# The last eleven token scatters of a routed-expert loop, spread over 22 tiles and not over 16

## The chip, the cores and the metric

The kernel runs on one core of one Trainium2 chip. The metric is device time in microseconds (us) of one execution. Three runs of the kernel before took 496.35, 493.66 and 497.1 us, a median of 496.35 us. The profile is of one further execution.

## What is computed

The reference is one decoder layer on 64 x 64 tokens of width 128: self-attention with 8 heads, an mLSTM cross step against a context, and a mixture-of-experts feed-forward, each added to its input and normalised. The change touches the last of them alone, which is:

```python
for i in range(E_SHARED):
    shared_out = shared_out + _expert(x, shared_up[i], shared_down[i])
probs = jax.nn.softmax(jnp.einsum('bsh,he->bse', x, router_w), axis=-1)
top_k_prob, top_k_idx = jax.lax.top_k(probs, K)          # K = 2 of 8 experts
onehot = jax.nn.one_hot(top_k_idx, E_ROUTED, dtype=x.dtype)
gates = jnp.einsum('bsk,bske->bse', top_k_prob, onehot)
for e in range(E_ROUTED):
    y = _expert(x, routed_up[e], routed_down[e])         # gelu(x @ up) @ down
    routed_out = routed_out + gates[..., e:e + 1] * y
return shared_out + routed_out + x
```

All tensors are float32; an expert's weights are 128x512 and 512x128.

## The kernel before

The 4096 tokens are 32 tiles of 128. Each token goes to two experts, so there are 8192 token copies. The kernel sorts them by expert through memory. **Scatter** n (n from 0 to 63, function `scatter`, line 471) is one indirect DMA from GpSimd (POOL in the profile): it takes the 128 rows of token tile n // 2 (130 numbers each: the token, its gate and its destination; from `tkr`, or from a copy in `zbuf` for odd n) and writes them to their places in a buffer `slots` in device memory. It raises one of four semaphores `scat`, by the quarter of the tokens it belongs to. Scatters 0 to 52 are issued in the stages ahead, the last of them during the shared expert. The remaining eleven, 53 to 63, belong to the last quarter and are issued inside the routed loop.

The **routed loop** runs over 71 expert tiles (`SLOT_TILES`), each 128 rows of `slots` that belong to one expert. A table worked out from the counts of the first half of the tokens picks the first 24 tiles (`EARLY`) so that they hold tokens of scatters 0 to 31 alone. The other 47 need all scatters. The engines do for tile t:

- SyncE (SP): wait until the row scatter of tile t - 8 has landed (semaphores `sc_y`), read the tile's place from a table, load 128 rows of `slots` into one of eight buffers `xr` (they lie in `zbuf`; lines 338 and 339). Ahead of tile 24 it waits at line 360 for all 16 scatters of each of the last two quarters.
- TensorE (PE): step t is a transpose of tile t (`turn`, line 1315, into `pair` or a bank), then four up matmuls of tile t - 1 (`up`, line 1323), then four down matmuls of tile t - 2 (`down`, line 1333), in this order. Each float32 matmul is two in the trace, hence x8. `turn` of tile t waits for the load of tile t.
- VectorE (DVE): copy the expert's up weights to `wst` (line 1802; `prob` in the trace), copy the transposed tile out (line 1795), then scale the output of tile t - 2 by its gates (`y_out`, line 1808). The up matmuls of a tile need the first two.
- ScalarE (ACT): gelu (line 894), which the down matmuls need.
- GpSimd: once `y_out` of tile t is done, the **row scatter** of tile t (`rows_out`, line 574), an indirect DMA of 128 rows of 128 numbers to `routed`.

GpSimd executes in the order of the program. So the order of row scatters and token scatters on it is what the Python code writes out: a straight part of 16 tiles (`2 * NX`, NX = 8), then a hardware loop for the rest. After the loop the final stage reads `routed`, adds and normalises.

Of the kernel before, what the change touches and what calls it, by code (L numbers as in the profile page):

```python
# [14 lines left out]
NT = B * S // P  # L15
# [10 lines left out]
SLOT_TILES = FILL_TILES - 1  # L26
EARLY = 24
IN_B = 21
IN_LOOP = IN_B + 32
# [38 lines left out]
def decoder_layer(nc, x, ctx_in, w_qk, w_v, w_out, b_out, conv, w_ig, b_ig, w_fg, b_fg, ln_w,  # L68
# [153 lines left out]
    NX = 8  # L222
# [160 lines left out]
    def _(pool):  # L383
# [81 lines left out]
        def scatter(n):  # L465
            t, k = n // 2, n % 2
            g = t // GT
            if n % (2 * GT) == 0:
                pool.wait_ge(s["slot_ok"], g // 2 + 1)
                pool.wait_ge(s["tk_ok"], 16 * (g + 1))  # L470
            pool.indirect_dma_start(slots, bass.IndirectOffsetOnAxis(ap=slot[:, k, t:t + 1], axis=0),  # L471
                                    (tkr, tk1)[k][:, t, :], None).then_inc(scat[g // 2], 16)
# [99 lines left out]
        def rows_out(t, n):  # L572
            pause(pool, s["y_ok"], t + 1, s["passed_pool"])
            pool.indirect_dma_start(routed, bass.IndirectOffsetOnAxis(ap=xr[n][:, :].bitcast(I32)[:, DEST:DEST + 1], axis=0),  # L574
                                    yr[n % 4][:, :], None).then_inc(sc_y[n % 4], 16)
        for t in range(2 * NX):
            rows_out(t, t % NX)
            if t % 3 < 2 and IN_LOOP + t - t // 3 < 2 * NT:
                scatter(IN_LOOP + t - t // 3)
        with pool.Fori(2, SLOT_TILES // NX) as i:  # L580
            for n in range(NX):
                rows_out(NX * i + n, n)
        for n in range(SLOT_TILES % NX):
# [1312 lines left out]
```

## Time and profile before

| | |
|---|---|
| median of three runs | 496.35 us |
| profiled execution | 495.9 us, of which the span from first to last instruction is 493.7 us |
| TensorE, matmul busy | 459.5 us, 93% |
| VectorE | 309.5 us, 63% |
| ScalarE | 277.9 us, 56% |
| GpSimd | 184.8 us, 37% |
| mean granted TensorE clock | 0.977 of full |

The page of the profile gives for each engine the busy time. The engine names are PE (matmul), PEld (its weight loads, which run beside matmuls), DVE, ACT, POOL and SP. The routed loop lies between about 305 and 467 us of the span. All times below are us from the span's start.

### The profile page before, as it was taken

To read this page: it belongs to the slowest core of one execution; us is meant where nothing else is said; L and a number is where in the kernel's file an instruction comes from. 1 tells how busy PE (TensorE), PEld (TensorE's weight loads), DVE (VectorE), ACT (ScalarE), POOL (GpSimd) and SP (SyncE) were. 2 spreads that over 40 slices of the span, in tenths; PEclk is the share of its full clock that TensorE was granted. 3 is DMA by queue.
4 is the path that set the end of the run, shared out by engine and by line. 5 is a ranking of instruction groups with operands and counts; after the bars stand their busy time and mean duration, and the time that the engine had idled before them with its cause. 6 is when DMAs were issued, how large, how long until landed. Compare 5 with 4: busy or idle time off the path is not lost.

```text
span 493.7 us, 15314 instructions
## 1 busy us (share of the span) xinstructions
PE 459.5 (93%) x5214; PEld 389.1 (79%) x5215; DVE 309.5 (63%) x1002; ACT 277.9 (56%) x624; POOL 184.8 (37%) x209
## 2 busy tenths in 40 slices
PE   8999999999998999989889999788899999999984
PEld 7688888887786777766579999777799999999631
DVE  5578888888885678888665672333344544455246
ACT  5687867786666989887678542112122332222226
POOL 5512011117000111156656464565545555555300
PEclk9999999999998999999979999898899999999999
DMA  5343136500000161111112123121222222222186
GB/s 140 88 120 99 53 97 132 156 1 4 24 5 19 37 222 45 45 50 56 56 56 70 39 70 90 58 63 60 60 67 65 65 65 69 59 70 60 53 288 203
DMA packets 47879, 37.98 MB, mean 77 GB/s; under 512 B 5456, under 2 KB 41184, under 8 KB 47824
## 3 DMA queue, kind: packets, MB, share of 16 engines
q1 hardware_dynamic: 43072, 28.10, 20.8%
q0 software_dynamic: 4320, 8.92, 5.1%
q8 instruction: 37, 0.61, 0.5%
q10 hardware_dynamic: 432, 0.20, 0.1%
q14 instruction: 18, 0.15, 0.1%
HBM read 19.30 MB, written 16.34 MB: 72 GB/s over the span
## 4 chain that ended last, share of the span: by engine, by line
PE 55%; DVE 21%; ACT 9%; issue 7%; DMA 3%; another core or an unknown queue 2%; DVEq 2%; SPq 0%; POOL 0%; ACTq 0%; POOLq 0%
PE bank L1333 12%; PE bank L1323 12%; PE bank L1283 6%; DVE tkr L1445 2%; DVE negmax L1454 2%; DVE prob L1451 2%; PE bank L1007 2%; PE bank L954 2%; DMA wdn<-routed 2%; PE bank L956 2%; PE bank L955 2%; PE bank L997 2%; PE pair L1315 1%; DVE stats L1593 1%
## 5 line engine op out<-in xcount | busy, mean ns | idle before, releaser
L894 ACT ACTIVATE prob<-bank 128x512 f32<-128x512 f32 x71 | 42.2, 597 | 121.3 <-PE bank L1323 106.8
L574 POOL DMA_INDIRECT routed<-zbuf x71 | 73.6, 1036 | 72.1 <-DVE zbuf L1808 40.3
L1323 PE MATMUL bank<-cT,prob 128*128 128x128 f32 x568 | 78.9, 283 | 8.9 <-DVE prob L1802 7.9
L1333 PE MATMUL bank<-wdn,prob 128*128 x568 | 80.6, 287 | 1.7 <-ACT prob L894 1.5
L1323 PEld LDWEIGHTS bank<-cT,prob 128*128 128x128 f32 x568 | 71.2, 197 | 12.2 <-DVE prob L1802 9.9
L1333 PEld LDWEIGHTS bank<-wdn,prob 128*128 128x128 f32 x568 | 71.4, 197 | 2.9 <-issue 2.2
L1802 DVE COPY prob<-wup 128x512 f32 x71 | 30.6, 430 | 44.6 <-issue 25.4
L1808 DVE TENSOR_SCALAR zbuf<-bank,zbuf 128x128 f32<-128x128 f32 x71 | 24.9, 350 | 46.0 <-PE bank L1333 29.6
L471 POOL DMA_INDIRECT slots<-zbuf,slot x32 | 31.4, 981 | 20.8 <-PE bank L1283 7.6
L471 POOL DMA_INDIRECT slots<-tkr,slot x32 | 31.5, 986 | 13.9 <-issue 6.4
L461 POOL TENSOR_TENSOR hlw<-hst,lnw 128x512 f32<-128x512 f32 x8 | 10.2, 1275 | 63.2 <-ACT hst L784 63.2
L1283 PEld LDWEIGHTS bank<-sdn,qblk 128*128 128x128 f32 x256 | 30.1, 194 | 0.6
L1283 PE MATMUL bank<-sdn,qblk 128*128 128x128 f32 x256 | 30.1, 277 | 0.0
L607 ACT ACTIVATE prob<-prob 128x512 f32<-128x512 f32 x32 | 20.2, 631 | 14.7 <-DVE prob L1455 14.6
L954 PE MATMUL bank<-xT_hi,wq_hi 128*128 128x512 f32 x64 | 27.9, 436 | 0.0
L1180 PEld LDWEIGHTS bank<-vals,cmat 64*64 64x64 f32 x512 | 17.6, 134 | 10.4 <-issue 10.4
L956 PE MATMUL bank<-xT_lo,wq_hi 128*128 128x512 f32 x64 | 25.4, 397 | 0.0
L955 PE MATMUL bank<-xT_hi,wq_lo 128*128 128x512 f32 x64 | 25.1, 393 | 0.0
L1451 DVE TENSOR_TENSOR prob<-pair,bias 128x512 f32<-128x512 f32 x32 | 22.0, 688 | 4.0 <-PE pair L977 2.7
L1455 DVE TENSOR_TENSOR prob<-prob,negmax 128x512 f32<-128x512 f32 x32 | 23.3, 728 | 1.1
L1160 PE MATMUL bank<-qblk,cT 128*64 128x256 f32 x128 | 21.0, 405 | 2.5 <-DVE cmat L1554 1.9
L1180 PE MATMUL bank<-vals,cmat 64*64 64x33 f32 x512 | 20.7, 222 | 2.8 <-issue 2.2
(281 smaller groups left out, 995.0 us busy)
## 6 DMA issues: line engine op xcount, KB each, us to landing
slots<-x2T SPq DMA_DIRECT2D x8, 585.0 KB, 5.3
zbuf<-slots SPq DMA_DIRECT2D x71, 65.0 KB
tkr<-in_x SPq DMA_DIRECT2D x8, 256.0 KB, 2.9
cs<-in_ctx SPq DMA_DIRECT2D x8, 256.0 KB, 2.8
wup<-in_L_ffn_routed_up SPq DMA_DIRECT2D x1, 2048.0 KB, 8.7
zbuf<-tkr SPq DMA_DIRECT2D x8, 256.0 KB
wup<-routed SPq DMA_DIRECT2D x8, 256.0 KB, 3.6
wdn<-routed SPq DMA_DIRECT2D x8, 256.0 KB, 4.0
```

The source lines that it names most:

```text
L471: pool.indirect_dma_start(slots, bass.IndirectOffsetOnAxis(ap=slot[:, k, t:t + 1], axis=0), (tkr, tk1)[k][:, t, :], None).then_inc(scat[g ...
L574: pool.indirect_dma_start(routed, bass.IndirectOffsetOnAxis(ap=xr[n][:, :].bitcast(I32)[:, DEST:DEST + 1], axis=0), yr[n % 4][:, :], None) ...
L894: act.activation(hT[:, n % 2, :], bank[2 + n % 2][:, :], ACT.Gelu).then_inc(s["hT_ok"], 1)
L954: mm(bank[4 + h % 2][:, :], wq_hi[:, h, :], xh[:, :], start=True, stop=False)
L955: mm(bank[4 + h % 2][:, :], wq_lo[:, h, :], xh[:, :], start=False, stop=False)
L956: mm(bank[4 + h % 2][:, :], wq_hi[:, h, :], xl[:, :], start=False, stop=True).then_inc(s["z_ps"], 1)
L1180: m = mm(bank[5 + k // 2][r, c:c + 33], cmat[r, k % 2, h * S:(h + 1) * S], vals[q][r, k, h, :], start=True, stop=True)
L1283: m = mm(bank[4 + g % 2][:, k * D:(k + 1) * D], shT[g % 2][:, c, k * P:(k + 1) * P], sdn[:, c, :], start=(c == 0), stop=(c == FC - 1))
L1323: m = mm(bank[2 + n % 2][:, c * P:(c + 1) * P], wst[:, n % 2, c * P:(c + 1) * P], xrT[:, n % 2, :], start=True, stop=True)
L1333: m = mm(bank[6 + n % 2][:, 0:D], hT[:, n % 2, c * P:(c + 1) * P], wdn[:, bass.ds(e * (FC * D) + c * D, D)], start=(c == 0), stop=(c == FC ...
L1451: tt(prob[:, k, :].rearrange("p (e x) -> p e x", e=2), pair[:, :, 0:256], bias[:, :, :].rearrange("p (e c) j -> p e (c j)", e=2), ALU.add) ...
L1802: dve.tensor_copy(wst[:, n % 2, :], wup[:, bass.ds(e * FF, FF)]).then_inc(s["wst_ok"], 1)
```

## The change

The straight part of the GpSimd program is 24 tiles long, and a token scatter stands behind the row scatters of tiles 0, 2, 4, ... 20. Before, it was 16 tiles long with token scatters behind the row scatters of tiles 0, 1, 3, 4, 6, 7, 9, 10, 12, 13 and 15. The scatters, their number and their data are the same.

```diff
-        for t in range(2 * NX):
+        for t in range(3 * NX):
             rows_out(t, t % NX)
-            if t % 3 < 2 and IN_LOOP + t - t // 3 < 2 * NT:
-                scatter(IN_LOOP + t - t // 3)
-        with pool.Fori(2, SLOT_TILES // NX) as i:
+            if t % 2 == 0 and IN_LOOP + t // 2 < 2 * NT:
+                scatter(IN_LOOP + t // 2)
+        with pool.Fori(3, SLOT_TILES // NX) as i:
```

What stands in the GpSimd program at the start of the routed loop, before (-) and now (+). L574 is a row scatter, L471 a token scatter; "x2" is two in a row.

```order
 L574 DMA routed<-zbuf 9344x128 [waits y_ok]
 L471 DMA slots<-zbuf,slot 43008x130
-L574 DMA routed<-zbuf 9344x128 [waits y_ok]
+L574 DMA routed<-zbuf 9344x128 [waits y_ok] x2
 L471 DMA slots<-tkr,slot 43008x130
 L574 DMA routed<-zbuf 9344x128 [waits y_ok] x2
 L471 DMA slots<-zbuf,slot 43008x130
```

Before, a pair of token scatters had one row scatter between them and two ahead of the next pair. Now two row scatters stand between any two token scatters. The same at the last two token scatters, 62 and 63:

```order
-L574 DMA routed<-zbuf 9344x128 [waits y_ok]
+L574 DMA routed<-zbuf 9344x128 [waits y_ok] x2
 L471 DMA slots<-tkr,slot 43008x130
 L574 DMA routed<-zbuf 9344x128 [waits y_ok] x2
 L471 DMA slots<-zbuf,slot 43008x130
+L574 DMA routed<-zbuf 9344x128 [waits y_ok] x3
 L580 UNCONDITIONAL_BRANCH
```

The last row but two was behind tile 15's row scatter and is now behind tile 20's; three row scatters (21 to 23) follow ahead of the hardware loop. The program of SyncE is the same in both. This is its place between tile 23 and tile 24 (rows of the changed kernel), where the last token scatter is waited for:

```order
L339 DMA zbuf<-slots 128x130
L341 REGISTER_ALU
L341 COMPARE_AND_BRANCH
L341 UNCONDITIONAL_BRANCH [waits scat2,scat3,st_pad,toff_ok]
L341 ISA
L338 ISA [waits sc_y0]
```

The load ahead of the wait is that of tile 23, and the one behind it is tile 24's; the wait did not move, but one of the things it waits for did.

## Rows read from the trace of the kernel before

**Rows 1.** Timeline, DVE, line 1808 (y_out), tiles 1, 2, 4, 6, 16, 20, 70.

```profile
310.38 0.35 DVE L1808 TENSOR_SCALAR zbuf<-bank,zbuf 128x128 f32<-128x128 f32 x1 [0.43 <-PE bank L1333]
...
315.34 0.35 DVE L1808 TENSOR_SCALAR zbuf<-bank,zbuf 128x128 f32<-128x128 f32 x1 [3.46 <-PE bank L1333]
...
320.02 0.35 DVE L1808 TENSOR_SCALAR zbuf<-bank,zbuf 128x128 f32<-128x128 f32 x1 [2.15 <-PE bank L1333]
...
325.65 0.35 DVE L1808 TENSOR_SCALAR zbuf<-bank,zbuf 128x128 f32<-128x128 f32 x1 [1.39 <-PE bank L1333]
...
355.18 0.35 DVE L1808 TENSOR_SCALAR zbuf<-bank,zbuf 128x128 f32<-128x128 f32 x1 [2.58 <-issue]
...
363.04 0.35 DVE L1808 TENSOR_SCALAR zbuf<-bank,zbuf 128x128 f32<-128x128 f32 x1 [0.45 <-PE bank L1333]
...
463.47 0.35 DVE L1808 TENSOR_SCALAR zbuf<-bank,zbuf 128x128 f32<-128x128 f32 x1 [1.00 <-PE bank L1333]
```

**Rows 2.** Stretches: from:to, length; busy PE, PEld, DVE, ACT, POOL; clock, DMA share, GB/s.

```profile
296.00:310.00 14.00, 13.63 (x115) 13.15 (x114) 4.22 (x11) 3.75 (x7) 6.34 (x8) 1.00 0.34 86
310.38:355.18 44.80, 35.74 (x257) 34.00 (x256) 14.54 (x46) 8.74 (x15) 26.10 (x27) 0.89 0.20 60
355.18:463.47 108.29, 107.19 (x909) 104.23 (x908) 51.38 (x158) 32.94 (x54) 55.53 (x54) 1.00 0.22 63
317.70:321.10 3.40, 3.40 (x19) 3.40 (x18) 0.75 (x3) 0.60 (x1) 1.92 (x2) 0.50 0.26 80
```

**Rows 3.** Timeline, POOL: start us, length us, instruction, idle time before it and releaser.

```profile
310.90 0.96 POOL L471 DMA_INDIRECT slots<-zbuf,slot  x1 [0.31 <-DVE zbuf L1808]
312.17 0.96 POOL L574 DMA_INDIRECT routed<-zbuf  x1 [0.30 <-issue]
313.43 0.96 POOL L471 DMA_INDIRECT slots<-tkr,slot  x1 [0.30 <-issue]
...
321.16 0.96 POOL L574 DMA_INDIRECT routed<-zbuf  x1 [1.07 <-issue]
322.43 0.95 POOL L471 DMA_INDIRECT slots<-tkr,slot  x1 [0.30 <-issue]
323.69 1.21 POOL L574 DMA_INDIRECT routed<-zbuf  x1 [0.30 <-issue]
326.79 1.07 POOL L574 DMA_INDIRECT routed<-zbuf  x1 [1.90 <-DVE zbuf L1808]
```

**Rows 4.** Timeline, PE, around tiles 2 to 10.

```profile
311.18 1.06 PE L1333 MATMUL bank<-wdn,prob 128*128 x8
...
316.91 1.36 PE L1323 MATMUL bank<-cT,prob 128*128 128x128 f32 x8 [2.67 <-DVE prob L1802]
...
326.18 1.15 PE L1333 MATMUL bank<-wdn,prob 128*128 x8 [0.69 <-ACT prob L894]
```

**Rows 5.** Groups by line, DVE alone, 310.38 to 355.18 and 355.18 to 463.47.

```profile
L1802 DVE COPY prob<-wup 128x512 f32 x15 | 6.5, 436 | 8.1 <-issue 8.1
...
L1802 DVE COPY prob<-wup 128x512 f32 x52 | 22.3, 429 | 34.6 <-PE bank L1323 18.4 <-issue 16.1
```

**Rows 6.** Timeline, POOL: token scatter 63, row scatters of tiles 16 and 20.

```profile
353.74 0.95 POOL L471 DMA_INDIRECT slots<-zbuf,slot  x1 [0.30 <-issue]
356.32 1.06 POOL L574 DMA_INDIRECT routed<-zbuf  x1 [1.63 <-DVE zbuf L1808]
...
364.18 1.06 POOL L574 DMA_INDIRECT routed<-zbuf  x1 [0.96 <-issue]
```

**Rows 7.** SP: line 360 (duration min/median/max ns, starts), and the load of tile 24.

```profile
L360 SPq EVENT_SEMAPHORE  x2: 17/22/28, 356.1 to 356.4; - x2
...
359.55 0.26 SPq L339 DMA_DIRECT2D zbuf<-slots  x1
```

**Rows 8.** Issues of DMAs: KB, median us from issue to landing.

```profile
wv<-in_L_attn_W_v ACTq DMA_DIRECT2D x1, 64.0 KB, 1.9
```

**Rows 9.** Timeline, PE: the transpose of tile 24.

```profile
364.66 0.28 PE L1315 MATMUL pair<-ident,zbuf 128*128 128x128 f32 x1
```

## The prediction

> **What bounds the kernel now.** I read the busy time by stretch first. From 355.18 to 463.47 TensorE is busy for 107.19 of 108.29 us at the full clock (1.00, which is 2.4 GHz): the routed loop is bound by TensorE [rows 2]. The starts of y_out give its pace: tile 16 at 355.18 and tile 70 at 463.47, 54 tiles in 108.29 us, 2.0 us each [rows 1]. From 310.38 to 355.18, tiles 1 to 16, it is not: TensorE is busy for 35.74 of 44.80 us at a mean clock of 0.89 [rows 2]. Fifteen tiles at 2.0 us would take 30.1 us, so **14.7 us are lost** there. They split into 9.1 us without a matmul (44.80 - 35.74) and the half clock: a mean of 0.89 means 22% of the stretch at 0.5 (1.2 GHz), 9.9 us, in which half the work is done, 4.9 us. The row of 317.70 to 321.10 is one of three such pieces, and it follows the wait of 2.67 us before 316.91 [rows 2, 4]. This stretch is the one in which GpSimd has token scatters between its row scatters: 27 DMAs for 16 tiles.
>
> The timelines show how the two hang together. GpSimd starts DMAs 1.26 us apart when it never waits (310.90, 312.17, 313.43; 321.16, 322.43, 323.69) [rows 3]. Before the change five of them fall on three tiles: 6.3 us of GpSimd for 6.0 us of TensorE, so it is overbooked. And in such runs the consumers learn late that TensorE is done. Tile 2's down matmuls, from 311.18 for 1.06 us, end at 312.24, but y_out of tile 2 starts at 315.34 after 3.46 us of idle time put down to just these matmuls [rows 1, 4]. The next weight copy stands behind it on VectorE, and TensorE then waits 2.67 us for that copy. What holds the signal back the profile doesn't name. Ahead of the loop, where token scatters have gaps, TensorE is busy for 13.63 of 14.00 us [rows 2]. So the loss comes with runs of GpSimd DMAs without a gap, or with the token scatters among them; which, the change will tell.
>
> **The change part by part.** Nothing is added or removed; eleven DMAs of about 1 us move. Two terms follow.
>
> *Term 1, the stretch with scatters.* Three DMAs for two tiles are 3.8 us of GpSimd for 4.0 us of TensorE: it just keeps up. But each group is still a row scatter, a token scatter and a row scatter without a gap. Such a group exists before: 321.16, 322.43, 323.69, then a gap of 1.90 us [rows 3]. From y_out of tile 4 to that of tile 6 it takes 5.63 us where two tiles take 4.0: 1.6 us lost, of which TensorE shows 0.69 as a wait [rows 1, 4]. The rest may be left from the half clock just before, so the price of one group lies between 0.69 and 1.6; I take the middle, 1.15. Below 0.69 the bound is nothing at all, if the group was only hit because GpSimd came to it late; above, 1.6. Ten groups cost 11.5 us; the eleventh falls into the wait of term 2. Term 1 is 11.5 - 14.7 = **-3.2 us**.
>
> One rule of the Trainium skill bears on the cause. "SBUF — State Buffer", section "Who interferes with whom", says that a VectorE copy in a two-port mode and GpSimd lock each other out for a whole instruction, descriptor writing included. If that were the loss, each scatter would hold one weight copy for up to its own 1 us, the count of scatters being the same the loss would stay, and the sum would be that of the rival "as costly as now". By the rows the copies are not held: 436 ns in the stretch with token scatters and 429 ns in the one without [rows 5].
>
> *Term 2, tile 24.* SyncE waits ahead of the load of tile 24 for all token scatters. Before, scatter 63 starts at 353.74 and the wait at line 360 ends at 356.4, 2.7 us later; the load isn't held by it, since it waits for tile 16's row scatter anyway (356.32) and goes out at 359.55, 3.2 us after that started [rows 6, 7]. Now scatter 63 stands behind tile 20's row scatter. With y_out of tile 20 as zero: its row scatter starts at 1.14 (363.04 to 364.18), scatter 63 at 2.40 (1.26 later), the load goes out 3.2 us after (the same chain of landing, table read and issue), at 5.6, and lands 1.9 us later, by the nearest row of 64 KB, at 7.5 [rows 1, 3, 6 to 8]. The transpose of tile 24 stood at 364.66 - 363.04 = 1.6 [rows 1, 9]. It is late by **5.9 us**. It stands first in step 24, so the up matmuls of tile 23 and the down matmuls of tile 22 wait behind it although their data is there, and then gelu, y_out and the row scatters. Nothing hides it: TensorE has no idle time behind it in which to catch up [rows 2]. The loads of tiles 25 to 28 are late too, but by then their row scatters have landed and SyncE issues them in a row; I take it that each comes ahead of its 2.0 us and adds nothing. The wait is longer than the 2.67 us that was followed by 3.4 us at half clock, so I add one such piece, **1.7 us**. Term 2 is **+7.6 us**. Its bounds: the load may land in less (1.9 is a transfer at the kernel's start, 1.5 possible, an estimate), and the clock may not fall or fall for two pieces: 5.5 to 9.3.
>
> In "DMA: Bandwidth & Descriptors", section "Anatomy of one DMA — SWDGE (gpsimd) path", the Trainium skill gives a GpSimd DMA about 2.0 us plus bytes / 436e3, an estimate of 2.15 us for these 66,560 bytes. By it tile 24 would be late by some 0.5 us less; the row's 2.7 us decides.
>
> *Sum.* The profiled execution took 495.9 us (span 493.7), 0.45 below the median of 496.35. 495.9 - 3.2 + 7.6 = **500.3 us**.
>
> **The rivals.**
> *Relief, the other side.* If GpSimd's being overbooked is the sole cause, then 3.8 us in 4.0 us ends it, no group costs anything, and the whole 14.7 us come back: 495.9 - 14.7 + 7.6 = **488.8 us**, faster. For it: where token scatters had gaps TensorE did not wait. Against: the group at 321.16 came after a gap of 1.07 us and had its loss nonetheless [rows 3]. It decides from a price below some 0.2 us a group: 14.7 - 10 x 0.2 - 7.6 = 5.
> *Half relief.* A group costs the 0.69 us that TensorE shows: 495.9 - 14.7 + 6.9 + 7.6 = **495.7 us**, no change.
> *As costly as now.* Each token scatter costs what it does now, 14.7 / 11 = 1.34 us, wherever it stands: -14.7 + 13.4 + 7.6 gives **502.2 us**; at 1.6 us a group 504.8.
> *The wait at tile 24 is hidden.* Were TensorE so late by the groups that tile 24's load had come, term 2 would vanish: 492.7 us. Against it: what delays TensorE delays y_out of tile 20, from which the 7.5 us count. So hardly.
>
> **How the numbers follow.** Forecast 0.37 (497 to 502), as costly as now 0.27 (to 505), half relief 0.19 (493 to 497), relief 0.13 (487 to 492), hidden wait 0.04. The likeliest gives 500.3. The range reaches into relief and over the costly case: 490 to 506. A measurement of this kernel can tell about 1% from no change, so the borders are 491.4 and 501.3. Slower takes most of the costly case and a third of the forecast: 0.38. Faster takes relief and a bit of the hidden wait: 0.16. Same keeps 0.46.
>
> **What would show it.** In the changed profile TensorE must have one wait of 5 to 6 us ahead of the transpose of tile 24, ended by the load, whose issue comes about 3.2 us after token scatter 63; after it a piece at clock 0.50. Between y_out of tiles 1 and 20 the time over 2.0 us a tile must be near 11 us, without pieces at half clock, in waits of about 1 us, one for each token scatter. If it is near 0, relief is right and GpSimd's booking is the cause; if near 13 or more with pieces at half clock, the token scatters themselves cost. No wait at tile 24 would make term 2 wrong, and with it the sign.

## The result, and the profile after

The changed kernel took 498.9 us (median of 20 runs) beside 494.1 us for the kernel before (20 runs): a ratio of **1.0083, 95% interval 1.0059 to 1.0108**. It is slower, by 4.8 us between the medians (4.1 us by the ratio), where the prediction had +4.4; 498.9 us lies between the borders of 491.4 and 501.3 us within which the prediction counted a time as no change. The ratio leaves out three runs of the changed kernel that lay over 1.5% above its fastest. The profiled execution has a span of 497.4 us where before had 493.7.

Starts of y_out (line 1808) of tiles 1, 20, 23 in the changed kernel's timeline of VectorE; they answer to [rows 1]:

```profile
310.51 0.35 DVE L1808 TENSOR_SCALAR zbuf<-bank,zbuf 128x128 f32<-128x128 f32 x1 [0.43 <-PE bank L1333]
...
359.88 0.35 DVE L1808 TENSOR_SCALAR zbuf<-bank,zbuf 128x128 f32<-128x128 f32 x1 [1.25 <-PE bank L1333]
...
374.07 0.35 DVE L1808 TENSOR_SCALAR zbuf<-bank,zbuf 128x128 f32<-128x128 f32 x1 [0.48 <-PE bank L1333]
```

From tile 1 to tile 20 it takes 49.37 us; before took 363.04 - 310.38 = 52.66 us [rows 1]. So the stretch with token scatters is **3.3 us shorter**. Then the sign turns. The busy time by stretch, cut at these tiles and at tile 70 (467.31); from:to, length, busy PE, PEld, DVE, ACT, POOL, clock, DMA share, GB/s, as in [rows 2]:

```profile
310.51:359.88 49.37, 39.08 (x327) 37.08 (x326) 18.09 (x57) 11.24 (x19) 28.22 (x30) 1.00 0.20 60
359.88:374.07 14.19, 7.92 (x52) 7.70 (x51) 3.03 (x10) 1.79 (x3) 4.74 (x5) 0.76 0.18 52
374.07:467.31 93.24, 92.66 (x790) 90.29 (x789) 44.57 (x138) 28.77 (x47) 48.35 (x48) 1.00 0.22 63
365.50:372.30 6.80, 4.44 (x21) 4.41 (x22) 1.01 (x3) 0.60 (x1) 0.83 (x1) 0.50 0.24 60
```

The first stretch has TensorE idle for 10.3 of 49.37 us, all of it at the full clock. The second has three tiles in 14.19 us. The last one is bound by TensorE, as before. The fourth row is the piece at half clock (0.50) inside the second stretch. From tile 20 to tile 70 it takes 107.43 us where before took 463.47 - 363.04 = 100.43 us [rows 1]: **7.0 us longer**. The two add up to +3.7 us, which is the difference of the spans. All of the 7.0 us and a little more arises in the three tiles: before took 6.61 us from tile 20 to tile 23 (y_out of tile 23 starts at 369.65 in its trace) and 93.82 us from there to tile 70, now it is 14.19 and 93.24 us, so +7.6 and -0.6 us.

The row that makes the second stretch is in the timeline of TensorE, the transpose of tile 24, answering to [rows 9]:

```profile
367.86 0.47 PE L1315 MATMUL pair<-ident,zbuf 128*128 128x128 f32 x1 [6.27 <-DMA zbuf<-slots]
368.12 2.03 PE L1323 MATMUL bank<-cT,prob 128*128 128x128 f32 x8
369.95 1.92 PE L1333 MATMUL bank<-wdn,prob 128*128 x8
```

It waited 6.27 us for a load, and the eight matmuls behind it take 2.03 and 1.92 us where they take 1.06 at the full clock [rows 4]. The chain of work that ended last, in the order of time (start, length, what), tells where the load was:

```profile
361.02 1.07 POOL routed L574
362.09 0.30 issue
362.40 2.33 DMA slots<-zbuf,slot
...
364.75 0.03 SPq L360
...
365.82 1.91 DMA zbuf<-slots
...
367.86 0.47 PE pair L1315
```

It is the chain of the prediction link by link: tile 20's row scatter, token scatter 63, its landing, the wait at line 360, the load, the transpose. In the waits of SyncE (line, what it waited for: us in total, times, longest) line 360 had 0.3 us before and now has:

```profile
SPq L360 <- DMA slots<-zbuf,slot: 11.2, 1, 11.2
```

The first stretch looks like this on GpSimd; the rows answer to [rows 3]:

```profile
315.22 0.95 POOL L574 DMA_INDIRECT routed<-zbuf  x1 [1.96 <-DVE zbuf L1808]
316.48 0.96 POOL L471 DMA_INDIRECT slots<-tkr,slot  x1 [0.30 <-issue]
317.75 0.96 POOL L574 DMA_INDIRECT routed<-zbuf  x1 [0.31 <-issue]
319.86 0.96 POOL L574 DMA_INDIRECT routed<-zbuf  x1 [1.14 <-issue]
321.12 0.99 POOL L471 DMA_INDIRECT slots<-zbuf,slot  x1 [0.30 <-issue]
322.41 0.96 POOL L574 DMA_INDIRECT routed<-zbuf  x1 [0.30 <-issue]
```

Groups of three, 1.26 us apart, each followed by a gap. And TensorE has a wait for nearly every group; that of the second group is

```profile
320.43 1.15 PE L1323 MATMUL bank<-cT,prob 128*128 128x128 f32 x8 [0.75 <-DVE cT L1795]
```

There are eight such waits of 0.59 to 2.17 us for the ten groups, 10.3 us together.

### The profile page after: what moved, and what is told of

It reads as the page before. It is cut to its first block, busy times and chain, and to the rows that moved or that the text cites. A ratio compares the mean times of both kernels' runs of the same rounds, so it can differ in the third digit from the quotient of the medians.

```text
span 497.4 us, 15304 instructions
## 1 busy us (share of the span) xinstructions
PE 457.9 (92%) x5214; PEld 386.6 (78%) x5215; DVE 309.6 (62%) x1002; ACT 278.4 (56%) x624; POOL 184.2 (37%) x209
## 4 chain that ended last, share of the span: by engine, by line
PE 54%; DVE 19%; ACT 9%; issue 7%; DMA 5%; another core or an unknown queue 2%; DVEq 2%; POOL 1%; SPq 1%; ACTq 0%; POOLq 0%
PE bank L1323 12%; PE bank L1333 11%; PE bank L1283 6%; DMA wdn<-routed 3%; DVE negmax L1454 2%; DVE prob L1451 2%; PE bank L1007 2%; PE bank L954 2%; DVE tkr L1445 2%; PE bank L956 2%; PE bank L955 2%; PE bank L997 2%; PE pair L1315 1%; DVE prob L1455 1%
## 5 line engine op out<-in xcount | busy, mean ns | idle before, releaser
L574 POOL DMA_INDIRECT routed<-zbuf x71 | 73.2, 1031 | 76.1 <-DVE zbuf L1808 48.5
L1323 PE MATMUL bank<-cT,prob 128*128 128x128 f32 x568 | 77.7, 281 | 8.9 <-DVE prob L1802 5.6
L1333 PE MATMUL bank<-wdn,prob 128*128 x568 | 78.8, 282 | 2.3 <-ACT prob L894 2.2
L1323 PEld LDWEIGHTS bank<-cT,prob 128*128 128x128 f32 x568 | 70.1, 194 | 12.3 <-DVE prob L1802 7.3
L1333 PEld LDWEIGHTS bank<-wdn,prob 128*128 128x128 f32 x568 | 69.7, 193 | 3.3 <-issue 2.7
L471 POOL DMA_INDIRECT slots<-zbuf,slot x32 | 31.5, 985 | 21.2 <-PE bank L1283 7.6
L471 POOL DMA_INDIRECT slots<-tkr,slot x32 | 31.2, 976 | 13.6 <-issue 6.3
L607 ACT ACTIVATE prob<-prob 128x512 f32<-128x512 f32 x32 | 20.2, 631 | 14.7 <-DVE prob L1455 14.6
L1315 PE MATMUL pair<-ident,zbuf 128*128 128x128 f32 x71 | 19.6, 279 | 6.3 <-DMA zbuf<-slots 6.3
```

What stands on the lines that cost most here:

```text
L1323: m = mm(bank[2 + n % 2][:, c * P:(c + 1) * P], wst[:, n % 2, c * P:(c + 1) * P], xrT[:, n % 2, :], start=True, stop=True)
L1333: m = mm(bank[6 + n % 2][:, 0:D], hT[:, n % 2, c * P:(c + 1) * P], wdn[:, bass.ds(e * (FC * D) + c * D, D)], start=(c == 0), stop=(c == FC ...
```

## The experiments

One thing has to be told ahead, since no number below can be read without it. The runs were made in several sessions, and the kernel before took 494 us in some and 477 us in others, within about 1% of its median inside a session (but for one run of it of 1475.66 us, beside extra_gaps). In the runs behind the prediction and the comparison above it took 494 to 496. I call the first the *slow condition* and the second the *quick condition*. All times are compared within their session. Nothing on record says what sets the condition; it is not the chip's number, since chip 9 showed both. There is no trace of the kernel before in the quick condition, so its order is read there from kernels that share it. The two conditions turned out to be an experiment of their own.

### Only the last scatter moved

The kernel before, with scatter 63 behind tile 20 and not behind tile 15:

```diff
-        for t in range(2 * NX):
+        at = [0, 1, 3, 4, 6, 7, 9, 10, 12, 13, 20]
+        for t in range(3 * NX):
             rows_out(t, t % NX)
-            if t % 3 < 2 and IN_LOOP + t - t // 3 < 2 * NT:
-                scatter(IN_LOOP + t - t // 3)
-        with pool.Fori(2, SLOT_TILES // NX) as i:
+            if t in at:
+                scatter(IN_LOOP + at.index(t))
+        with pool.Fori(3, SLOT_TILES // NX) as i:
```

> The order of before, except that the last token scatter, 63, stands behind tile 20's row scatter and not behind tile 15's. Two-term theory: the wait at tile 24 comes by this one move. TensorE waits 5.5 to 6.5 us ahead of the transpose of tile 24, followed by one or two pieces at half clock, and the kernel takes 6 to 8 us more than before, less the 1.3 us that scatter 63 costs at tile 15: +5 to +7 us. Rival (the wait at tile 24 is made by all eleven scatters being late, or by the longer straight part of the GpSimd program): less than 2 us more than before.

Measured, quick condition: 485.5 beside 477.15 us, ratio 1.0185 (1.0131 to 1.0239), +8.4 us (four runs of this kernel). TensorE's timeline at the transpose of tile 24 (its line is 1316 here):

```profile
355.10 0.47 PE L1316 MATMUL pair<-ident,zbuf 128*128 128x128 f32 x1 [6.33 <-DMA zbuf<-slots]
```

The busy time of each engine in two stretches of the same kernel, tiles 1 to 16 and the piece behind the wait (columns as above):

```profile
308.99:339.08 30.09, 30.09 (x258) 29.38 (x257) 14.87 (x45) 8.96 (x15) 22.77 (x25) 1.00 0.29 81
...
355.10:359.90 4.80, 4.80 (x22) 4.76 (x23) 0.64 (x2) 0.60 (x1) 0.00 (x0) 0.50 0.24 56
```

The wait comes by this one move. The size was missed upwards: 4.8 us at half clock behind it are 2.4 us, and the 1.3 us that I had taken off for scatter 63 were not there. The first stretch says why: fifteen tiles in 30.09 us, with TensorE never idle, in the *order of before* but for scatter 63. The 14.7 us lost there by [rows 1, 2] are absent in the quick condition.

### The changed kernel in the quick condition

> The changed kernel itself beside before, on whatever chip this runs. In the last runs before took 477 us where it took 494 to 496 in the runs of the comparison, and no TensorE signal came late there, before's fifteen tiles 1 to 16 taking 2.0 us each. Theory: the 14.7 us lost in the stretch with token scatters belong to the chip or its state, and the wait at tile 24 belongs to the order. So where before takes some 477 us, the changed kernel takes 6 to 8 us more (1.3 to 1.7%), all of it at tile 24, and where before takes some 495 us it takes 3 to 5 more (0.6 to 1.0%). Rival (both terms change together by the chip): the ratio is 1.008 in either case.

Measured: 485.1 beside 476.7 us, ratio 1.0173 (1.0135 to 1.021), +8.4 us (four runs), a little above the expected 6 to 8. The stretches of this kernel from tile 1 to 20 and from 20 to 23:

```profile
309.21:346.99 37.78, 37.78 (x326) 37.03 (x325) 18.73 (x58) 11.35 (x19) 28.29 (x30) 1.00 0.27 79
346.99:360.54 13.55, 7.54 (x52) 7.29 (x51) 3.03 (x10) 1.79 (x3) 4.41 (x5) 0.75 0.20 54
```

The transpose of tile 24 in its timeline of TensorE:

```profile
354.75 0.47 PE L1315 MATMUL pair<-ident,zbuf 128*128 128x128 f32 x1 [6.01 <-DMA zbuf<-slots]
```

So the two terms separate. The wait at tile 24 belongs to the order and is there in both conditions. The loss at token scatters, and with it all that the spacing can win, belongs to the slow condition. The rival with one ratio for both is out: the intervals of 1.0173 and 1.0083 don't touch.

### The spacing without the wait

Against the changed kernel ("..." marks lines left out, here and below):

```diff
+        for n in range(2):
+            scatter(IN_LOOP + n)
+        at = list(range(0, 17, 2))
...
-            if t % 2 == 0 and IN_LOOP + t // 2 < 2 * NT:
-                scatter(IN_LOOP + t // 2)
+            if t in at:
+                scatter(IN_LOOP + 2 + at.index(t))
```

> Two token scatters (53, 54) go out ahead of tile 0's row scatter, where GpSimd idles for 3.6 us, and the other nine behind the row scatters of tiles 0, 2, ... 16. So the spacing is that of the changed kernel but the last scatter is out by tile 16. Two-term theory: no wait at tile 24; nine groups at about 1.15 us are 10 us where 14.7 us were lost before: -4 to -5 us against before (-0.9%). Relief theory (GpSimd overbooked is all): no loss, -14 us. Rival that spacing gains nothing: within 1 us of before less two scatters' 1.3 us each, -2.6 us.

Measured, quick condition: 476.7 beside 477.15 us, ratio 0.9984 (0.9959 to 1.0009): no difference. With nothing lost at token scatters there is nothing to win: its tiles 1 to 16 take 29.88 us. With the last one at tile 16 there is no wait: from y_out of tile 20 (346.95) to that of tile 23 (353.53) it takes 6.58 us, where before took 6.61 and the changed kernel 13.55 in this condition. The expectation of -4 us was made without the condition in mind and fell with it.

### How far back the last scatter may stand

The kernel before, with scatter 63 behind tile 18. The edit is that of last_at_20 with another last number:

```diff
+        at = [0, 1, 3, 4, 6, 7, 9, 10, 12, 13, 18]
...
```

> As last_at_20, but scatter 63 stands behind tile 18's row scatter. Every tile is 2.0 us, so the wait ahead of the transpose of tile 24, 6.3 us with the scatter at tile 20, is to be 4.0 us shorter: 2.3 us, with about one piece at half clock after it at most. Two-term theory: +2 to +4 us against before, and the wait ends by the load of tile 24. Rival (the wait isn't a chain from scatter 63 but a fixed cost of the scatter being in the third group of eight tiles): 6 us of wait again.

Measured, slow condition: 497.4 beside 494.4 us, ratio 1.0035 (0.9994 to 1.0076), an interval that holds 1: the times alone tell no difference, and the trace carries this one. The transpose of tile 24 in its timeline of TensorE:

```profile
370.02 0.33 PE L1316 MATMUL pair<-ident,zbuf 128*128 128x128 f32 x1 [1.90 <-DMA zbuf<-slots]
```

Two tiles earlier, the wait is 1.90 us where it is 6.0 to 6.3, so 4.1 to 4.4 us shorter for 4.0 us of two tiles. It is a chain from the scatter, not a fixed cost. By the same slope of 2.0 us a tile it would be gone with the scatter at tile 17; that is an estimate and was not run.

### The clock behind the wait

The changed kernel, with 26 matmuls that nobody reads (a filler) ahead of the loop from tile 24 on:

```diff
         pe.wait_ge(s["toff_ok"], 2)
+        pe.wait_ge(s["base_ok"], NG)
+        filler(4, 26)
```

> The changed kernel with 26 identity matmuls of 128 x 128 into an unused bank ahead of the transpose of tile 24, some 5.8 us of TensorE work that lies in the wait for the load and computes nothing that is used. The wait itself stays (the tile comes when the load does), but TensorE has no idle time in it. If the half clock behind the wait is a cost of its own: 1.7 to 2.4 us less than the changed kernel, which takes 8.4 us more than before on this chip, so +6 to +7 us. If the half clock costs nothing: +8.4 us or more.

Measured, slow condition: 497.6 beside 494.4 us, ratio 1.0064 (1.0033 to 1.0094). The filler is 5.97 us of TensorE work at line 932. TensorE's timeline between tile 20 and the transpose of tile 24:

```profile
359.05 5.97 PE L932 MATMUL bank<-ident 128*128 128x128 f32 x52
366.08 0.33 PE L1315 MATMUL pair<-ident,zbuf 128*128 128x128 f32 x1 [1.06 <-DMA zbuf<-slots]
366.31 1.15 PE L1323 MATMUL bank<-cT,prob 128*128 128x128 f32 x8
```

The stretch of this kernel from y_out of tile 20 to that of tile 23:

```profile
358.28:370.52 12.24, 11.18 (x97) 10.72 (x96) 2.93 (x10) 1.80 (x3) 3.63 (x4) 1.00 0.18 51
```

12.24 us where the changed kernel has 14.19, and the clock stays at 1.00. The transpose starts 7.80 us after y_out of tile 20 and not 7.98, so 0.2 us of the difference is a load that came sooner, and the half clock behind the wait is a cost of its own of some 1.8 us; the rest of term 2 is the wait. The expected +6 to +7 us was reckoned from the quick condition. Here it is +3.1 us, where the comparison had +4.8; the ratio, against 1.0083, points the same way, but the two intervals overlap; the trace carries this one. From tile 1 to tile 20 this kernel takes 49.25 us, against 49.37 in the changed kernel's own profile: term 1 repeats.

### All token scatters ahead, without gaps

Against the kernel before: every scatter from a point ahead of the shared expert on stands there in one row, without the waits between them, and none is left in the loop.

```diff
-        first = IN_B
-        pool.wait_ge(s["shu_ps"], FC + 2)
-        scatter(first)
-        pool.wait_ge(s["x2T_ps"], NG - 1)
-        scatter(first + 1)
...
-        pool.wait_ge(s["shd_ps"], NG)
-        scatter(IN_LOOP - 1)
+        for n in range(IN_B, 2 * NT):
+            scatter(n)
...
-        for t in range(2 * NX):
-            rows_out(t, t % NX)
-            if t % 3 < 2 and IN_LOOP + t - t // 3 < 2 * NT:
-                scatter(IN_LOOP + t - t // 3)
-        with pool.Fori(2, SLOT_TILES // NX) as i:
+        with pool.Fori(0, SLOT_TILES // NX) as i:
```

> All token scatters from 21 on without waits on TensorE's progress between them, one behind the other at 1.26 us from about 255 us on; the eleven late ones are out before tile 0's row scatter. Where TensorE's signals don't come late (before at some 477 us): nothing to win in the loop, which runs at 2.0 us a tile already, and nothing lost, within 2 us of before; if GpSimd isn't done when tile 0 is, its row scatter is late by a few us and the first tiles wait, +1 to +4 us. Where they come late (before at some 495 us): the loop wins 14 us, and the shared expert ahead of it loses 5 us or more.

Measured, slow condition: 522.1 beside 494.4 us, ratio **1.0554** (1.0489 to 1.0619). The busy time in three stretches of this kernel, the shared expert's first and second part, then tiles 1 to 16:

```profile
255.00:309.00 54.00, 34.93 (x203) 28.91 (x202) 14.18 (x48) 20.43 (x33) 26.58 (x28) 0.73 0.12 39
309.00:350.71 41.71, 31.35 (x219) 28.71 (x218) 16.15 (x53) 9.28 (x16) 16.59 (x17) 0.88 0.20 52
350.71:380.48 29.77, 29.77 (x258) 29.32 (x257) 14.71 (x45) 8.98 (x15) 15.62 (x16) 1.00 0.23 66
```

The kernel before over nearly the same time:

```profile
255.00:308.00 53.00, 52.63 (x397) 48.97 (x396) 28.72 (x97) 28.88 (x47) 31.09 (x33) 0.99 0.23 65
```

There TensorE is busy nearly without a break; in this kernel it is idle for a third of the time. The third row is the other half of the finding: with no token scatter left in it, the loop runs its fifteen tiles in 29.8 us, in the slow condition. From 255.46 on GpSimd issues 27 token scatters in a row; its timeline at one place:

```profile
281.02 0.96 POOL L471 DMA_INDIRECT slots<-zbuf,slot  x1 [0.30 <-issue]
282.28 0.96 POOL L471 DMA_INDIRECT slots<-tkr,slot  x1 [0.30 <-issue]
```

TensorE's timeline just behind it:

```profile
284.42 0.58 PE L1201 MATMUL pair<-wq_hi,xT_hi 128*128 128x512 f32 x1 [2.44 <-issue]
288.05 0.59 PE L1202 MATMUL pair<-wq_hi,xT_lo 128*128 128x512 f32 x1 [3.05 <-issue]
290.84 0.59 PE L1203 MATMUL pair<-wq_lo,xT_hi 128*128 128x512 f32 x1 [2.20 <-issue]
```

And ScalarE's, for the instruction that reads what these matmuls wrote:

```profile
293.99 1.09 ACT L837 ACTIVATE qblk<-pair 128x512 f32<-128x512 f32 x2 [8.80 <-PE pair L1203]
```

GpSimd issues without a gap, and three matmuls that add into the same bank, with no wait between them in the code, start 3.6 and 2.8 us apart, with "issue" before them, which says that the profile knows nothing they waited for. ScalarE idles for 8.80 us, from 285.19 on. For 6.2 us of it TensorE itself is late, since the third of these matmuls ends only at 291.43 (290.84 + 0.59); the other 2.6 us pass between that end and ScalarE's start.

A late signal shows more clearly near the head of the same row, in one instruction of VectorE, the copy of the router's result. In the code it waits for the router's matmuls. First in the kernel before, then here, where those matmuls lie 0.24 us later:

```profile
261.25 0.19 DVE L1573 COPY lg<-bank 128x32 f32<-128x32 f32 x1 [4.34 <-PE bank L1195]
...
266.93 0.19 DVE L1552 COPY lg<-bank 128x32 f32<-128x32 f32 x1 [9.82 <-remote]
```

The matmuls end at 261.12 (260.08 + 1.04) and at 261.36 (260.32 + 1.04). The copy starts 0.13 us after that where GpSimd had just paused for 1.14 us, and 5.6 us after it in the row without a pause.

How long the row is matters too. Before issues token scatters 1.26 to 1.46 us apart in three rows of four between 255.18 and 271.96, in the same slow condition, and TensorE is busy for all of 20.00 us from 255 to 275. In this kernel it is busy for all of 10 us from 255 to 265, for 2.46 of the next 5 and for 1.12 of the 5 after. So the 1.1 to 1.4 us that a group costs in the routed loop is not a cost of any scatter, nor of any few of them close together: it depends on the stage, and it grows with the row. That the shared expert hides a late signal, having other matmuls to go on with, would explain it and is not shown. Nor was this kernel run in the quick condition. The expected "5 us or more" in the shared expert is some 40 us there (tile 1's y_out is at 350.71 and not at 310.38), against 15 us won in the loop, as expected.

### Gaps between the DMAs of a group

The order of spread_ahead2, with a small GpSimd memset on either side of each token scatter of the loop:

```diff
+                pool.memset(gap[:, 8 * t:8 * t + 4], 0.0)
                 scatter(IN_LOOP + 2 + at.index(t))
+                pool.memset(gap[:, 8 * t + 4:8 * t + 8], 0.0)
```

> spread_ahead2 (two token scatters ahead of the loop, nine behind the row scatters of tiles 0 to 16) with a small GpSimd memset ahead and behind each of the nine, so that the DMAs of a group start about 1.56 us apart and not 1.26. Where before takes some 495 us: the distance decides whether TensorE's signals are held, so if it does, tiles 1 to 16 take 2.0 to 2.2 us each and the kernel is 10 to 14 us faster than before; if it is the number of DMAs in the run whatever their distance, nine groups cost 1.15 us each and it is 4 to 5 us faster, as spread_ahead2 would be. Where before takes some 477 us: within 1 us of before.

Measured, slow condition: 491.6 beside 494.1 us, ratio **0.9947** (0.9918 to 0.9977). The question wasn't answered, since the memsets didn't do what they were there for, as its timeline of GpSimd shows:

```profile
311.58 0.12 POOL L583 MEMSET gap<- 128x4 f32 x1
311.88 0.97 POOL L472 DMA_INDIRECT slots<-zbuf,slot  x1 [0.19 <-DVE zbuf L1814]
312.84 0.13 POOL L585 MEMSET gap<- 128x4 f32 x1
313.15 0.97 POOL L575 DMA_INDIRECT routed<-zbuf  x1 [0.19 <-issue]
```

They lie in the 0.30 us that are idle between two DMAs anyway, and the DMAs stand 1.27 us apart. So this is in effect spread_ahead2 in the slow condition, and as such it is of use: nine groups and two scatters ahead, without the wait at tile 24. It is 2.6 us faster than the kernel before, less than the expected 4 to 5, and the interval of its ratio lies below that of the changed kernel. Its tiles 1 to 16 take 40.76 us (before: 44.80 [rows 2]):

```profile
311.30:352.06 40.76, 33.22 (x266) 31.73 (x265) 14.39 (x45) 8.87 (x15) 25.66 (x40) 0.96 0.21 62
```

### Other GpSimd work in the clean part of the loop

Two kernels, in the order of before, with extra work behind every second row scatter of tiles 26 to 68; for that the GpSimd program is written out for all 71 tiles. The first:

```diff
...
+            if 26 <= t <= 38 and t % 2 == 0:
+                at_slots(spare_y, made, total_in[:, made, :])
+                made += 1
+            if 42 <= t <= 54 and t % 2 == 0:
+                at_slots(spare, made, tkr[:, made, :])
+                made += 1
+            if 58 <= t <= 68 and t % 2 == 0:
+                pool.memset(gap[:, 8 * made:8 * made + 4], 0.0)
+                at_slots(spare, made, tkr[:, made, :])
+                pool.memset(gap[:, 8 * made + 4:8 * made + 8], 0.0)
+                made += 1
```

`at_slots` is an indirect DMA of GpSimd to a spare buffer that nobody reads, with rows of 512 bytes in the first place and of 520 in the others.

> The order of before, and 20 extra indirect DMAs of GpSimd in the clean part of the loop, one behind every second row scatter, each to a spare buffer that nobody reads: tiles 26 to 38 rows of 512 bytes as the row scatters have (7), tiles 42 to 54 rows of 520 bytes as the token scatters (7), tiles 58 to 68 the same with a small GpSimd memset ahead and behind, which widens the distance between DMAs (6). GpSimd's DMAs without a gap are the cause: all of the first two kinds cost 1.0 to 1.3 us for each, alike (7 to 9 us per stretch), and the third less, if the distance matters. Token scatters as such are the cause (their rows, or slots being read at the same time): the first kind costs under 0.3 us, the second 1 us if it's the rows, and under 0.3 us too if it's slots.

> The kernel extra_a once more. Where before takes some 477 us: again nothing is lost at the 20 extra DMAs. Where before takes some 495 us: 1.0 to 1.3 us for each extra DMA of either kind if runs of GpSimd DMAs without a gap hold TensorE's signals back there, and under 0.3 us for the row kind if only token scatters do; less for those with a memset ahead and behind if the distance matters.

> The kernel extra_a a third time, for a run where before takes some 495 us and TensorE's signals do come late. What all_ahead showed there (token scatters one behind the other hold the signals for up to 12 us) leaves open whether it is token scatters or any GpSimd DMAs, and whether the distance decides. Any DMAs in a run: each row-kind extra (tiles 26 to 38) and each token-kind extra (42 to 54) costs 1.0 to 1.3 us, that is 2.5 us a tile. Token scatters alone: 2.0 us a tile in the first, 2.5 in the second. The distance decides: 2.0 to 2.2 us a tile for the third kind, with memsets between. Where before takes some 477 us all three stand at 2.0 again.

Measured three times, each time in the quick condition: 477.6, 481.7 and 476.7 us beside 477.15, 476.7 and 478.4. With one run each, and the second 5 us above its neighbour, the times tell little. The traces tell more: tiles 26 to 40 take 28.99, 28.90 and 28.39 us in the three, and 28.30 in changed_again, which has nothing extra there; tiles 42 to 56 take 28.48 each time, and 28.27 there. Seven DMAs cost 0.7 us at most, where 7 to 9 were expected if they were the cause. The second kernel had a plain DMA (`pool.dma_start`), a GpSimd multiply of 1.27 us, and an indirect DMA of 32 rows in the three places.

> The order of before, and other extra GpSimd work in the clean part of the loop, behind every second row scatter: tiles 26 to 38 a plain (not indirect) DMA of 128 x 520 bytes to a spare buffer (7), tiles 42 to 54 a GpSimd multiply of 1.27 us and no DMA (7), tiles 58 to 68 an indirect DMA of 32 rows only (6). If writing descriptors without a gap holds TensorE's signals back: 1.0 to 1.3 us for each plain DMA, 0 for each multiply, and less than 1 us for 32 rows. If it is GpSimd being busy that delays row scatters and so the loads: the multiply costs as much as a DMA.

Measured, quick condition, one run: 479.3 beside 477.15 us. The weight copies of VectorE (busy us, mean ns) in two stretches of the first kernel, tiles 26 to 40 and 42 to 56:

```profile
L1818 DVE COPY prob<-wup 128x512 f32 x14 | 6.7, 480 | 9.7 <-issue 6.6 <-PE bank L1339 3.2
...
L1818 DVE COPY prob<-wup 128x512 f32 x14 | 6.4, 460 | 9.6 <-PE bank L1339 4.8 <-issue 4.8
```

And in the second kernel from tile 42 to 56, with the multiplies:

```profile
L1819 DVE COPY prob<-wup 128x512 f32 x14 | 8.0, 572 | 9.2 <-issue 6.8 <-PE bank L1340 2.4
```

A GpSimd multiply stretches the copies from 429 [rows 5] to 572 ns on average, the indirect DMAs to 460 to 480. The traces agree in kind with the lock between a two-port VectorE copy and GpSimd that the Trainium skill states ("SBUF — State Buffer", section "Who interferes with whom"). By its size it is not the loss looked for: the DMAs add 30 to 50 ns a copy. The multiplies do cost something: with them tiles 42 to 56 take 30.03 us, 1.8 more than 28.27, about what fourteen copies 143 ns longer add up to.

The last kernel put the question once more, on spread_ahead2: first with DMAs of the row kind without gaps, then with real gaps around them (a small multiply ahead and behind), then with DMAs of the token kind. `gap` is the small multiply:

```diff
...
+            if t in (24, 27, 30, 33, 36):
+                at_slots(spare_y, made, total_in[:, made, :])
+                made += 1
+            if t in (42, 45, 48, 51, 54):
+                gap(gaps)
+                at_slots(spare_y, made, total_in[:, made, :])
+                gap(gaps + 1)
+                made, gaps = made + 1, gaps + 2
+            if t in (60, 63, 66):
+                at_slots(spare, made, tkr[:, made, :])
+                made += 1
```

> spread_ahead2 for tiles 0 to 23 (two token scatters ahead, nine behind tiles 0 to 16), and then 13 extra DMAs to spare buffers, one behind every third row scatter: tiles 24 to 36 five of the row kind without a gap, tiles 42 to 54 five of the row kind with a GpSimd multiply of 128 x 128 ahead and behind, which puts the DMAs some 1.6 us apart (the memsets of spread_gap fitted into the 0.30 us that lie between two DMAs and left them 1.27 us apart), tiles 60 to 66 three of the token kind without a gap. Where before takes some 495 us: any DMAs of GpSimd in a run cost about 1.3 us a group, so 2.4 us a tile in the first and the third stretch; if the distance decides, 2.0 to 2.1 us a tile in the second. Token scatters alone: 2.0 in the first. Where before takes some 477 us: 2.0 in all three.

Measured: 477.5 beside 476.8 us, ratio 1.0006 (0.9973 to 1.004), quick condition; tiles 24 to 36 take 2.03 us each, tiles 42 to 54 2.05 and tiles 60 to 69 1.92, where changed_again has 1.99, 2.02 and 1.91. By this it is left open whether token scatters or any DMAs of GpSimd hold the signals, and which distance is enough.

## Why the prediction was right, point by point

**The bound and the two terms.** Predicted 500.3 us from a profiled execution of 495.9, a rise of 4.4; the profiled execution of the changed kernel took 499.6. Measured is a rise of 4.8 between medians and 3.7 between spans. The loop is bound by TensorE behind tile 24, as said.

**Term 1** was -3.2 us and is -3.3. Its price of a group, 1.15 us from the middle between 0.69 and 1.6, met ten groups that lost 49.37 - 19 x 2.0 = 11.4 us. It was said that this would come in waits of about 1 us, one for each token scatter, without pieces at half clock. The clock is 1.00, and there are eight waits for ten groups. The mean over the eleven scatters of before, 1.34, has half clocks in it that the changed order escaped. Yet the closeness is in part luck: the price was the middle of a range whose ends are 9 us apart over ten groups. And the split of the 14.7 us into 9.1 and 4.9 leaves 0.7 without a name. spread_gap, with nine such groups, loses 50.14 - 38.0 = 12.1 us from tile 1 to tile 20, 1.35 us a group, with a wait of 2.25 us and a piece at half clock (the mean clock of 0.96 in its row). That the cause goes by the distance alone, as the gaps ahead of the loop suggested in the prediction, is not so: earlier in the shared expert of the kernel before there are rows of four without a gap that cost TensorE nothing.

**Term 2** was +7.6 us and is +7.0 by y_out of tiles 20 and 70. In the three tiles where it was to arise it is +7.6 us; the loop behind them gives 0.6 back. Its parts are less exact. The transpose was to be 5.9 us late and is 6.4: it stands 7.98 us behind y_out of tile 20 (367.86 - 359.88), where before had 1.6. The load goes out 3.4 us after scatter 63 starts (365.82 - 362.40), not 3.2, and the transpose 2.0 us after it, not 1.9. The half clock was one piece of 3.4 us, 1.7 us of loss; there are 6.8 us of it, the first part in the wait, and 4.44 us of work lie in it, 2.2 us of loss. fill_wait puts that loss at some 1.8. TensorE's wait of 6.27 us and the clock together are 8.5 us, and the three tiles take 14.19 - 6.0 = 8.2 more than their pace. Before itself was 0.6 us over its pace there (6.61), so the change adds only 7.6. So that the sum came out at 7.6 is in part luck: each part was some 0.5 us too small (5.9 and 1.7 against 6.4 and 2.2), and most of that was made up by the 0.6 us that before lost there already and the prediction had not counted; 0.3 to 0.4 us I can't place.

**The cause.** The prediction left open whether overbooked GpSimd or token scatters as such cost the time, with relief as the rival. Relief is out as the whole story: at 3.8 us of GpSimd in 4.0 us of TensorE the loss stays in the slow condition, and in the quick one the overbooked order of before loses nothing. "As costly as now" gave 502.2 us, 2.6 above the profiled execution. What the prediction did not see is that the loss has a condition. In the quick one the order of before (last_at_20) and the changed one run at 2.0 us a tile, so the whole of term 1 is zero there, and the change costs its full term 2, 1.7%. So the forecast of +4.4 us was right only because the comparison ran in the condition of the trace it was made from. In the slow one, TensorE's signals arrive late while GpSimd issues DMAs one behind the other, by 1 to 3 us in groups of three and four and by 5.6 us in a long row (all_ahead). In [rows 1, 4] it is 3.1 us, 312.24 to 315.34, and the engine named by the profile can be trusted there: y_out of tile 2 waits in the code for nothing but TensorE's semaphore. ScalarE, whose gelu waits for another semaphore of TensorE and for nothing else, is held up at the same moment, 2.2 us behind up matmuls that end at 313.24 (timeline of before):

```profile
315.46 0.60 ACT L894 ACTIVATE prob<-bank 128x512 f32<-128x512 f32 x1 [3.19 <-remote]
```

Shown is the going together, not the mechanism. What in the chip holds the signal, whether the late matmuls of all_ahead have the same cause, and what sets the condition, is open.

**The hidden wait** as a rival is out as well: what delays TensorE delays the scatter, so the wait was as long in the slow condition (6.27) as in the quick one (6.01).

## What to carry to other kernels

When work is spread out to make room, look for who waits for its last piece, and count the tiles from there: here eleven scatters spaced better won 3.3 us, and the last of them, five tiles later, lost 7.0 at one wait that had cost nothing until then (in the slow condition; in the quick one nothing was won). Move the end of a spread no further than the chain behind it allows (here tile 17, by the estimate from last_at_18), and take what doesn't fit to the front, as in spread_ahead2, which was 0.5% faster than the kernel before in the slow condition (as spread_gap) and level with it in the quick one. The waits of 6.0 to 6.3 us on TensorE cost about a third more than their length, by the half clock that followed them (1.8 to 2.4 us); the wait of 1.90 us in last_at_18 had none behind it, its next eight matmuls taking 1.15 us.

## What I had not expected of the hardware

- The same kernel took 477 us in some sessions and 494 us in others, 3.5% apart, each steady within about 1%. Most of the difference lies where GpSimd issues indirect DMAs close together: of the 14.4 us between the spans of the changed kernel in the two (497.4 and 483.0), 11.6 lie between tiles 1 and 20. Fifteen tiles of the loop took 30.1 us in one (last_at_20) and 44.8 us in the other (before), and a comparison of two orders of these DMAs gave 1.0173 in one and 1.0083 in the other.
- In the slow condition a row of 27 token scatters 1.26 us apart went with 34.93 busy us of TensorE in 54, with matmuls starting up to 3.6 us apart for no reason that the profile names. The first eight of them cost it nothing: it was busy for all of the 10 us from 255 to 265.
- One and the same VectorE copy started 0.13 us after the end of the matmuls it waits for when GpSimd had paused, and 5.6 us after it within such a row.
- A small GpSimd memset between two indirect DMAs is free: it takes 0.12 us within the 0.30 us between them, and leaves their distance at 1.27 us.
